# Row maxima of two cross attentions: high halves in two row groups, with two score banks in place of three

## The reference

```python
# attention 1
scores = jnp.einsum('bhtd,bhsd->bhts', Q, K) * scale
scores = jnp.where(mask, scores, jnp.float32(-jnp.inf))
attn = jax.nn.softmax(scores, axis=-1)
out = jnp.einsum('bhts,bhsd->bhtd', attn, V)
# attention 3
attn = jnp.einsum('bkhd,bnhd->bhkn', q, kmat) / DH
attn = jnp.where(full_mask[:, None, None, :], attn, -jnp.inf)
attn = jax.nn.softmax(attn.astype(jnp.float32), axis=-1).astype(q.dtype)
attn_out = jnp.einsum('bhkn,bnhd->bkhd', attn, v).reshape(b, k_len, H)
```

## Time and profile before

| | |
|---|---|
| median of three executions | 5259.54 us (5256.17 to 5262.85) |
| profiled execution | 5261.2 us |
| its span | 5259.4 us |
| TensorE busy | 4670.2 us (89%) |
| VectorE, ScalarE, GpSimd busy | 3684.5, 3029.1, 2161.0 us |
| groups of attention 1, first to last product of pass 2 | 1740.0 to 2414.5 us |
| groups of attention 3 | 3929.8 to 4802.8 us |

### The profile page before, as it was taken

How to read it: one execution, slowest core, us unless ns; L and a number is a source line. 1 busy time by engine, 2 the same in 40 slices (tenths; PEclk the granted TensorE clock), 3 DMA queues, 4 the chain that set the end, 5 groups by cost and what they waited for, 6 DMA issues and landing times. The chain is left out here.

```text
span 5259.4 us, 76538 instructions
## 1 busy us (share of the span) xinstructions
PE 4670.2 (89%) x29250; PEld 1681.2 (32%) x29250; DVE 3684.5 (70%) x4667; ACT 3029.1 (58%) x5554; POOL 2161.0 (41%) x977
## 2 busy tenths in 40 slices
PE   7978998987686999997899999996789999995999
PEld 2323433443232233332222222222333333331444
DVE  6749989997563877770699999993567777771421
ACT  5644344443552566663488888885436666665432
POOL 1226666665333578873000000000008888885000
PEclk9989999999797899998999999998889999998999
DMA  3353433434112333313111111112434232312100
GB/s 130 127 169 102 113 106 105 116 110 120 68 57 64 74 70 70 70 45 124 57 33 33 33 33 33 33 29 71 119 96 84 63 78 59 75 34 77 65 24 17
DMA packets 474871, 391.97 MB, mean 75 GB/s; under 512 B 175151, under 2 KB 372628, under 8 KB 474472
## 3 DMA queue, kind: packets, MB, share of 16 engines
q1 hardware_dynamic: 474496, 387.00, 26.9%
HBM read 246.50 MB, written 139.34 MB: 73 GB/s over the span
## 5 line engine op out<-in xcount | busy, mean ns | idle before, releaser
L3114 DVE TENSOR_REDUCE att_part<-att_scores 128x2 f32<-128x802 f32 x1024 | 953.3, 986 | 105.8 <-PE att_scores L2953 94.0
L3087 ACT ACTIVATE att_prob<-att_lower 128x512 f32<-128x512 f32 (+1 forms) x1664 | 882.8, 597 | 125.2 <-PE att_lower L2967 103.9
L3921 DVE TENSOR_REDUCE att_part<-att_scores 128x1 f32<-128x423 f32 x1280 | 675.9, 589 | 219.5 <-PE att_scores L3624 219.5
L3865 ACT ACTIVATE att_prob<-att_lower 128x512 f32<-128x512 f32 (+1 forms) x1088 | 563.4, 603 | 244.0 <-PE att_lower L3636 242.1
L3905 POOL TENSOR_TENSOR att_acc<-att_acc,att_prob 128x1024 f32<-128x1024 f32 (+2 forms) x240 | 671.2, 2797 | 52.1 <-ACT att_prob L3865 23.0
L2690 DVE TENSOR_REDUCE att_part<-att_scores 128x1 f32<-128x401 f32 x1024 | 515.7, 567 | 162.8 <-PE att_scores L2504 162.7
L1684 POOL TENSOR_TENSOR scan_z<-scan_r,scan_states 128x512 f32<-128x512 f32 x256 | 467.7, 1831 | 344.3 <-DVE scan_states L1761 337.4
L2629 ACT ACTIVATE att_prob<-att_scores 128x512 f32<-128x512 f32 (+1 forms) x832 | 431.1, 602 | 196.5 <-PE att_scores L2516 196.5
L2982 PE MATMUL att_lower<-att_prob,att_v 128*32 128x256 f32 (+1 forms) x6144 | 520.9, 411 | 19.7 <-issue 19.7
L3101 POOL TENSOR_TENSOR att_out<-att_sums_sb,att_spread 128x512 f32<-128x512 f32 x32 | 40.7, 1272 | 1163.0 <-DMA att_spread<-recips 1163.0
L2670 POOL TENSOR_TENSOR att_acc<-att_acc,att_prob 128x1024 f32<-128x1024 f32 (+2 forms) x176 | 449.8, 2555 | 69.5 <-ACT att_prob L2629 57.4
(11 more groups left out here) (485 smaller groups left out, 8197.3 us busy)
## 6 DMA issues: line engine op xcount, KB each, us to landing
v<-scan_val SPq DMA_DIRECT2D x96, 256.0 KB, 2.3
att_v<-v SPq DMA_DIRECT2D x32, 768.0 KB
att_spread<-recips SPq DMA_DIRECT2D x64, 256.0 KB
mix_plane<-in_mask SPq DMA_DIRECT2D x16, 800.5 KB, 8.1
att_k<-k1hi SPq DMA_DIRECT2D x32, 400.2 KB
att_k<-k3hi SPq DMA_DIRECT2D x32, 400.2 KB
scan_x<-in_ctx_t SPq DMA_DIRECT2D x12, 1024.0 KB, 5.5
o<-att_out SPq DMA_DIRECT2D x32, 256.0 KB
```

The lines of the kernel that those rows point to most:

```text
L3087: nc.scalar.activation(prob[g % NP][0:kw(kt), h, :], scores2[0:kw(kt), n % RING2, :], ACT.Exp).then_inc(exped, 1)
L3114: nc.vector.reduce_max(part[q % 2][:, :, ec, piece], scores1[:, bank["unit", p], :, 0:PIECE], AX.X).then_inc(reduced, 1)
L3865: nc.scalar.activation(prob[g % NP][0:kw(kt), h, :], scores2[0:kw(kt), n % RING2, :], ACT.Exp).then_inc(exped, 1)
L3921: nc.vector.reduce_max(part[q % 2][:, hc, piece:piece + 1], scores1[:, bank["piece", p], 0:PIECE], AX.X).then_inc(reduced, 1)
```

## The change

In attentions 1 and 3 alike:

- Pass 1 uses the high halves alone: 32 rows and the mask row, in buffers of their own (`QP`, `KP`), two buffers of each. Head 2e + a lies at partition 64a, so heads 0 and 2 at partition 0 and heads 1 and 3 at partition 64, and a **unit** is the pair of 33-row products of both sides into two neighbouring banks, with one reduction over both. A quad has 32 (40) units.
- `scores1` is a ring of two pairs, four banks. `RING2` goes from 3 to 2 banks.
- A group is issued as `shift` 0, 1; units; `mix`; units; `shift` 2, 3; `count`; units. Three slots share the units of a group.
- `NB` goes from 4 to 2 buffers of the full `Q` and `K`; the loads of pass 1 are made apart and first.
- In attention 3 `FIRST_TOO` and `LAST_TOO` hold one block each in place of three: 7 counts a quad, and GpSimd adds a third head in 2 blocks in place of 6.
- Code for attention 3 that `cross_attention` no longer needs goes.

```diff
-    UNITS = QUAD * C * PIECES
-    RING1, RING2, NB, NP = 3, 3, 4, 5
-    LEAD, TURN, LAG = 5, 6, 2
+    SIDES, EACH = 2, QUAD // 2
+    UNITS = EACH * C * PIECES
+    RING1, RING2, NB, NP = 2, 2, 2, 5
+    LEAD, TURN, LAG = 5, 3, 2
+    SLOTS = 3
...
-    FIRST_TOO, LAST_TOO = {13: ((5,), (8,)), 17: ((4, 8, 12), (6, 10, 14))}[NT]
+    FIRST_TOO, LAST_TOO = {13: ((5,), (8,)), 17: ((8,), (12,))}[NT]
...
+    def units_by(g, slot=SLOTS - 1):
+
+        return min(N * UNITS, AHEAD + (g * SLOTS + slot + 1) * UNITS // (NT * SLOTS))
...
-        scores1 = ph.ps("scores1", [P, RING1, T])
+        scores1 = ph.ps("scores1", [P, RING1, SIDES, T])
...
+                def load_pieces(s):
+                    i = s % 2
+                    rows = slice(s * P, (s + 1) * P)
+                    for a in range(SIDES):
+                        r, m = slice(64 * a, 64 * a + dh), slice(64 * a + dh, 64 * a + dh + 1)
+                        sp.dma_start(QP[i][r], w[f"q{layer}hi"][rows].rearrange("(e a d) t -> a d e t", a=SIDES, d=dh)[a]).then_inc(ploaded[i], 16)
+                        sp.dma_start(KP[i][r], w[f"k{layer}hi"][rows].rearrange("(e a d) t -> a d e t", a=SIDES, d=dh)[a]).then_inc(ploaded[i], 16)
+                        sp.dma_start(KP[i][m], w[f"km{layer}"][s // C, 0:EACH].unsqueeze(0)).then_inc(ploaded[i], 16)
...
-                        b = take(("piece", p), reduced, p + 1)
-                        nc.tensor.matmul(scores1[:, b, 0:PIECE], Q[i][0:TOP, h, c * P:(c + 1) * P], K[i][0:TOP, h, k0:k0 + PIECE],
-                                         start=True, stop=True).then_inc(scored, 1)
+                        b = take(("unit", p), reduced, p + 1)
+                        for a in range(SIDES):
+                            r = slice(64 * a, 64 * a + dh + 1)
+                            ins = nc.tensor.matmul(scores1[:, b, a, 0:PIECE], QP[i][r, e, c * P:(c + 1) * P], KP[i][r, e, k0:k0 + PIECE],
+                                                   start=True, stop=True)
+                        ins.then_inc(scored, 1)
...
-                        for h in range(QUAD):
-                            shift(s, kt, h)
-                            if issued < pieces_by(g):
-                                next(one)
-                                issued += 1
+                        shift(s, kt, 0)
+                        shift(s, kt, 1)
+                        units(units_by(g, 0))
                     if g >= LAG:
                         ms, mk = divmod(g - LAG, NT)
                         mix(ms, mk)
-                        if mk in counts_at:
-                            count(ms, counts_at[mk])
-                    while g < G and issued < pieces_by(g):
-                        next(one)
-                        issued += 1
+                    if g < G:
+                        units(units_by(g, 1))
+                        shift(s, kt, 2)
+                        shift(s, kt, 3)
+                    if g >= LAG and mk in counts_at:
+                        count(ms, counts_at[mk])
+                    if g < G:
+                        units(units_by(g, 2))
...
-                    nc.vector.reduce_max(part[q % 2][:, hc, piece:piece + 1], scores1[:, bank["piece", p], 0:PIECE], AX.X).then_inc(reduced, 1)
+                    pair = part[q % 2][:].rearrange("p (e a c) k -> p e a c k", e=EACH, a=SIDES)[:, e, :, c, piece]
+                    nc.vector.reduce_max(pair, scores1[:, bank["unit", p], :, 0:PIECE], AX.X).then_inc(reduced, 1)
```

More of the change, by code:

```diff
@@ L2352, in cross_attention @@
         ph = Phase(nc, ctx, f"att{layer}")
+        QP = [ph.sb(f"qp{i}", [P, EACH, T], F16) for i in range(2)]
+        KP = [ph.sb(f"kp{i}", [P, EACH, NK], F16) for i in range(2)]
         Q = [ph.sb(f"q{i}", [P, QUAD, T], F16) for i in range(NB)]
@@ L2466, in _ @@
                         send_top(s + 1)
+                    if s + 3 < N:
+                        sp.wait_ge(scored, (s + 2) * UNITS)
+                        load_pieces(s + 3)
                     if s:
@@ L2676, in _ @@
             def _(dve):
-                if latents:
-                    for i in range(NB):
-                        nc.vector.memset(K[i][MASK:MASK + 1, :, 0:latents], 0.0).then_inc(cleared, 1)
                 for i in range(2):
@@ L3405, in latents_and_attention @@
             stages = [("Wo2", x3[1]), ("q_w3", qk), ("k_w3", v), ("v_w3", x3[1])]
-        K += [ph.sb(f"k{i}", [P, QUAD, NK], F16) for i in range(2, NB)]
+        K += [ph.sb("k1", [P, QUAD, NK], F16)]
         V = [ph.sb(f"v{i}", [P, NT, P]) for i in range(2)]
@@ L3670, in _, with units @@
                 issued = j = 0
+                def units(upto):
+                    nonlocal issued
+                    while issued < upto:
+                        next(one)
+                        issued += 1
                 def group(pairs):
-                    nonlocal issued, j
+                    nonlocal j
                     if j >= RING0:
@@ L3678, in group @@
                     ins.then_inc(product, 1)
-                    while issued < pieces_at(j):
-                        next(one)
-                        issued += 1
+                    units(units_at(j))
                     j += 1
@@ L3715, in _ @@
                         if kt == 0:
+                            if s < NB:
+                                pe.wait_ge(fixed[s], 16 * 2)
+                            pe.wait_ge(loaded[s % NB], 16 * LOADS * (s // NB + 1))
                             pe.wait_ge(topsent[s % 2], 16 * (s // 2 + 1))
-                        for h in range(QUAD):
-                            shift(s, kt, h)
-                            if issued < pieces_by(g):
-                                next(one)
-                                issued += 1
+                        shift(s, kt, 0)
+                        shift(s, kt, 1)
+                        units(units_by(g, 0))
                     if g >= LAG:
```

232 lines of the change are left out of this document (129 added, 103 removed).

## The result

The changed kernel takes **5385.64 us**, median of four executions (5385.09 to 5389.10), against 5257.90 (5256.17 to 5262.85) before: ratio 1.0243, 95% interval 1.0225 to 1.0261. The profiled execution took 5385.92 us, its span is 5384.1 us, 124.7 more than before.

What follows compares the result with a forecast made beforehand. TensorE's list of work was taken to set the groups' periods. Longer groups and tails, +144 us, less 12 in the openings gave +132 us on 5261.2, 5393 us, stated as 5392; range 5355 to 5435.

Steps and rivals of the forecast that it cites:

- The ring of two: Groups without `count`: with two banks the second `shift` waits for the last exponential, 3.43 us a group, before 2.83.
- The chain from S2 to the next S1: From the third `shift` of a group through two exponentials to the second `shift` of the next: 1.66 us.
- The surcharge: Pass-1 units: each change between 64-row tiles and the full array costs TensorE 0.11 us, in either direction.
- The rival without it: Changes of tile mode in pass 1 are free: groups of 3.25 and 3.46 us, 5295 us; chance 0.18.
- With `count`: Groups with a `count`: the `count` fills the stall, 3.73 us a group, before 3.70.
- the `total`: Group with the `total`: it stands in the same place as a `count`, 3.73 us, before 4.12.
- Quads: Period of a quad: 46.4 us in attention 1, before 42.8; 60.7 us in attention 3, before 55.0.
- Tail: Last groups, without pass 1: 2.97 us without `count`, 3.04 with it; +3 us in attention 1, +4 in attention 3.
- Openings: Start of attention 1 and stretch ahead of attention 3: earlier loads and fewer, paired reductions, together -12 us.
- The whole: Sum over the kernel: 144 - 12 = +132 us on the profiled execution's 5261.2 us, 5393 us.
- Clock: Rival: stalls in the groups drop the granted clock to 1.2 GHz part of the time, 5490 us; chance 0.04.
- What would show it: Profile signs: TensorE idle before `shift`, released by exponentials, about 0.8 us in 60% of groups, some 230 us in all.

Runs made afterwards that it cites:

- attention 1 alone: Kernel before with attention 1 as in the change and attention 3 left as before: 5308.51 us, ratio 1.0085.
- the kernel with three banks: Changed kernel without `count`, the bank `den` given to the ring of the `shift` products, three banks instead of two: 5164.03 us, ratio 0.9829.

## Why the prediction was right

Forecast 5392, measured 5386. By its steps:

- **The ring of two**, 3.43 us a group, measured 3.44 us for most and 3.44 on average over the seven of a quad. Right in mechanism, shown from both sides: two banks alone slow the kernel before by 210 us, a third bank takes 0.47 us out of a group. That the size came out so well is luck: two errors met. The chain from S2 to the next S1 was taken as 1.66 us; the couple at 2003.86 has its second product at about 2004.36, so 1.58 (the record of the couple, 0.89 us, less that of one product, 0.39). And 0.82 units for every slot hid that the units are not even: of the seven groups of this kind in a quad of attention 1 five have three, which the forecast would have put at 3.53.
- **The surcharge** of 0.11 us, taken from the earlier trace rows beside fp32 products: 0.21 us for two slots. The rival without it is refuted. The Trainium skill, page TensorEngine Tiling (Array Packing), Key Properties, says that a change of the tiling mode drains TensorE; the trace agrees with a price at each change, 0.11 us, though no row shows the draining itself.
- **With `count`** 3.73, measured 3.62; **the `total`** 3.73, measured 4.24 in attention 1: "the `total` stands in the same place" failed. It takes a pair of `scores1` and stands behind the unit of the third slot, and with two pairs it waits there for a reduction (0.27 us idle). In attention 3, where its group has two units, it takes 3.64 us and doesn't wait. In a quad of attention 1 the two errors cancel, -5 x 0.11 + 0.51.
- **Quads** 46.4 and 60.7, measured 46.4 and 60.3. From first to last `shift` +56 and +88, measured +62.6 and +82.9. Of attention 1's surplus of 6.6 us the tail has 2.4 (below). The rest can lie in its first groups: they start 12 us earlier, and the granted clock is 0.50 until about 1743 us, for 16 us of groups (before from 1740 to 1746, for 6); by estimate that costs up to (16 - 6) / 2 = 5 us.
- **Tail** of attention 1, +3, measured 56.7 us from the last unit to the last `shift` against 51.3, +5.4. Its groups were cheaper than forecast (2.88, not 2.97), but something else came in ahead of them: the last maxima. TensorE's timeline there (L2507 transposes the maxima):

```profile
2409.82 0.37 PE L2507 MATMUL att_scores<-const_ident,att_top 128*16 128x128 f32 x1 [1.44 <-DVE att_top L2711]
2410.11 1.94 PE L2547 MATMUL att_sums<-att_prob,att_v 128*32 128x512 f32 x8
```

  1.44 us of idleness, then some 6 us at the lower clock (a `mix` takes 1.94 us in place of 1.06). The wait belongs to the kernel, the clock behind it to this execution: the profiles of the changed kernel with six counts and of attention 1 alone have the same wait of 1.44 us, the clock stays at 1.00 behind it, and the tail takes 53.9 us, +2.6.
- **Openings** -12, of which 9 in attention 1, measured -12.4 there and -4.0 ahead of attention 3. Mis-sized by 3 us: the seven loads fewer were worth 9.8 us (first unit at 1687.7 against 1697.5), not 7. What follows attention 3 is 4.4 us shorter; the sum had no term for it, and no run shows why.
- **The whole**: +56 + 88 - 12 forecast, +62.6 + 82.9 - 16.4 - 4.4 measured. The misses go both ways, and that only 7 us are left is luck to that extent.
- **Clock** as a rival: in the groups it stays at 1.00 and 0.99 in spite of a wait in each one without `count`. But it was nearer than its chance of 0.04 said: the same kernel without counts has stretches at 0.50 behind waits of 0.47 us and less. The Trainium skill, page TensorE: Matmul & The Clock Gate, A second HAM failure mode: psum-queue depth-cycling, says that frequent small idles of TensorE between groups of matmuls, while PSUM banks are cycled, make the clock oscillate; the kernel without counts agrees (mean 0.96 in attention 1), the changed one, at 1.00, doesn't.
- **What would show it.** "0.8 us in 60% of the groups, some 230 us" was half right: the groups and the releaser are the foretold ones, the size isn't. TensorE stands still for 0.55 us in such a group, by estimate 0.55 x (7 x 14.6 + 9 x 14.7) = 130 us in all. As idleness the trace shows 0.19 us of it between couples, the rest inside records, and 89 us in the two stretches.

## What to carry to other kernels

Before giving a bank of PSUM from one ring to another, write down the chain that a bank goes through (product, exponential, next product) and lay it against the work that TensorE has between two uses: the shorter ring costs the difference, once a group. Compare the list of TensorE with nothing waiting first; here halving what pass 1 streams saved almost nothing of it, since every lone 64-row pair between full-array products pays two changes of mode (0.11 us each, on 0.17 us for the pair). And work that can run on either engine belongs off the one that has no gap: a `count` taken from TensorE gave 0.85 us a quad until GpSimd reached 96%.

## What the runs showed that I had not expected

- **A wait can cost several times its length through the clock, but need not.** In the kernel with three banks 2.2 us of idle TensorE were followed by 18 us at the 1.2 GHz level, and in the tail of the changed kernel 1.44 us by about 6. But the same trace has a longer wait in front of the same `shift`, and there the clock is 1.00 ahead of it and behind it; the wait of 1.44 us, too, left it at 1.00 in two other profiles (see the tail above). TensorE's timeline of the three-bank kernel, and the stretch around it:

```profile
1891.69 0.59 PE L2535 MATMUL att_scores<-att_q,att_k 98*128 98x512 f16 x2 [2.34 <-issue]
```
```profile
1880.00:1900.00 20.00, 16.11 (x99) 3.95 (x98) 13.78 (x16) 13.52 (x27) 14.29 (x7) 1.00 0.50 114
```

  So the length of a wait doesn't decide by itself. Neither do the counts: waits of 0.2 to 0.5 us left the clock at 1.00 in the changed kernel and brought stretches of 0.50 without the counts, but the kernel with its units behind the last `shift`, which has all its counts, falls to 0.50 for about 3 us in four quads of attention 1 (at 2136, 2276, 2324 and 2371 us), each time behind a wait of 0.89 us that the other quads have as well, at 1.00. What decides stays open; no run varied it alone.
- **An fp32 product costs less behind its like.** `mix`, `count` and `total` take about 1.00 to 1.10 us each between fp16 products, but 0.88 when another of them follows; putting the `total` there was worth 0.34 us. The cause isn't shown. All three also lie in four column groups of 32, so a second one behind the first would save two changes between that tiling and another. It costs 0.87 us in place of 1.10, and 0.23 is twice the 0.11 of a change. No run separates the number format from the tiling.
- **Which group gets how many units is set by a division**, and in attention 1 it gives the `count` groups two and six of the other eight three. An average over slots gave the right sum and the wrong price for a `count`.
